# One transpose of 128x64 and eight row copies, in place of eight transposes of 128x8 and four copies

## What is computed

```python
xn = _layernorm(x, axis=-1)
q, k, v = split(xn @ W_attn + b_attn)          # 16 heads of 16
q = _apply_rope(q); k = _apply_rope(k)          # the angle goes by the head's number
att = einsum('bhqd,bhkd->bhqk', q, k) / 4.0
att = where(causal, att, -inf)
att = softmax(att, axis=-1)
s = einsum('bhqk,bhkd->bhqd', att, v) @ W_proj + b_proj
g = silu(silu(xn @ wg.T) * (xn @ wu.T) @ wd.T)  # int8 weights times 1/127
return x + s * g
```

## Time and profile before

| | us |
|---|---|
| three runs, median | 1255.55 |
| three runs, lowest and highest | 1254.56, 1260.43 |
| profiled execution, span from its first to its last instruction | 1257.5 |
| PE busy in the span | 1197.4 |
| DVE, ACT, POOL busy | 1013.0, 935.2, 693.3 |

### The profile page before, as it was taken

One profiled execution on the slowest core, in us unless ns is written; L12 is line 12 of the kernel. 1 busy time (PEld: TensorE's weight loads), 2 busy tenths in 40 slices (PEclk: granted clock), 3 DMA queues, 4 the chain that ended last, 5 costly groups with the idle time before them and its releaser, 6 DMA issues.

```text
span 1257.5 us, 29932 instructions
## 1 busy us (share of the span) xinstructions
PE 1197.4 (95%) x11324; PEld 558.3 (44%) x11324; DVE 1013.0 (81%) x2098; ACT 935.2 (74%) x1736; POOL 693.3 (55%) x863
## 2 busy tenths in 40 slices
PE   3889999999999999999999999999999999999986
PEld 2334444545345443544445453454445444454433
DVE  6678988888888888888888888888888888878732
ACT  4447777787877878778777878778787787778774
POOL 4527544395535937177453946369371874446472
PEclk9879999999999999999999999999999999999999
DMA  6140020401222120400204011221204002120101
GB/s 170 47 136 2 2 86 19 119 19 60 53 72 74 35 88 32 119 19 27 85 31 115 20 63 48 86 66 30 91 28 119 19 27 86 39 73 29 42 2 51
DMA packets 56004, 73.23 MB, mean 58 GB/s; under 512 B 8398, under 2 KB 34452, under 8 KB 55860
## 3 DMA queue, kind: packets, MB, share of 16 engines
q1 hardware_dynamic: 55848, 71.30, 18.9%
q10 hardware_dynamic: 12, 0.01, 0.0%
HBM read 44.96 MB, written 25.17 MB: 56 GB/s over the span
## 4 chain that ended last, share of the span: by engine, by line
PE 74%; POOL 10%; DVE 6%; issue 4%; ACT 4%; SPq 1%; DMA 1%; POOLq 0%; DVEq 0%; ACTq 0%
PE ring L854 31%; PE acc L845 17%; PE st L781 11%; PE ring L809 8%; PE ring L927 2%; DVE mx_a L1218 2%; POOL hf L1542 2%; PE ring L824 2%; ACT pexp L1055 2%; POOL hT L1551 1%; PE ring L864 1%; POOL xn L535 1%; PE ring L963 1%; POOL pexp L1512 1%; PE ring L942 1%
## 5 line engine op out<-in xcount | busy, mean ns | idle before, releaser
L1055 ACT ACTIVATE pexp<-st 128x512 f32<-128x512 f32 x1152 | 623.8, 598 | 124.0 <-PE st L781 123.3
L1218 DVE TENSOR_REDUCE mx_a<-ring 128x1 f32<-128x512 f32 (+2 forms) x960 | 536.8, 611 | 50.9 <-PE ring L809 26.0
L1512 POOL TENSOR_SCALAR_AFFINE_SELECT pexp<-pexp 128x512 f32<-128x512 f32 x256 | 158.4, 638 | 412.9 <-ACT pexp L1055 412.9
L845 PE MATMUL acc<-pexp,v_pad 128*17 128x512 f32 (+3 forms) x3072 | 303.7, 490 | 5.8 <-POOL pexp L1512 4.5
L809 PE MATMUL ring<-k_st,q_st 56*128 56x512 f16 (+4 forms) x1536 | 231.4, 326 | 13.3 <-POOL k_st L1641 3.4
L781 PE MATMUL st<-q_st,k_st 58*128 58x512 f16 (+3 forms) x1536 | 231.9, 331 | 6.1 <-ACT pexp L1055 3.4
L1218 DVE TENSOR_REDUCE mx_b<-ring 128x1 f32<-128x384 f32 (+2 forms) x448 | 210.4, 528 | 25.5 <-PE ring L824 24.7
L781 PEld LDWEIGHTS st<-q_st,k_st 58*128 58x128 f16 x1536 | 61.3, 93 | 265.2 <-ACT pexp L1055 173.4
L1542 POOL TENSOR_TENSOR hf<-ga,ups 128x512 f32<-128x512 f32 x96 | 122.4, 1275 | 42.0 <-issue 41.5
L845 PEld LDWEIGHTS acc<-pexp,v_pad 128*17 128x17 f32 x3072 | 61.9, 96 | 129.1 <-issue 105.7
L1551 POOL TENSOR_TENSOR hT<-hf,hT 128x512 f16<-128x512 f32 x96 | 111.4, 1161 | 3.4
(11 more groups left out here) (152 smaller groups left out, 1536.2 us busy)
## 6 DMA issues: line engine op xcount, KB each, us to landing
parts_scratch<-parts SPq DMA_DIRECT2D x32, 512.0 KB, 2.8
q_st<-parts_scratch SPq DMA_DIRECT2D x186, 64.0 KB, 2.2
k_st<-parts_scratch SPq DMA_DIRECT2D x186, 64.0 KB, 2.2
xo<-in_x SPq DMA_DIRECT2D x32, 256.0 KB, 2.9
out<-xo SPq DMA_DIRECT2D x32, 256.0 KB, 2.2
xn<-in_x SPq DMA_DIRECT2D x7, 1024.0 KB, 6.1
q_st<-mT SPq DMA_DIRECT2D x126, 4.0 KB
xn<-in_x SPq DMA_DIRECT2D x2, 512.0 KB, 6.2
```

Of the source, the lines that this page charges most:

```text
L845: mm = nc.tensor.matmul(acc[32 * j:32 * j + D + 1, CH - w:CH], v_pad[:, kb, GH * g + j, :], pexp[:, GH * (m % NSET) + j, at:at + w], start ...
L1055: nc.scalar.activation(pexp[:, GH * (n % NSET) + j, :], st[:, (GH * n + j) % NST, :], ACT.Exp, scale=1.0 / (QK_SCALE * np.sqrt(D))).then_i ...
L1218: top_ = nc.vector.reduce_max(dst, src, AX.X)
L1512: nc.gpsimd.affine_select(out=t, in_=t, compare_op=ALU.is_ge, fill=0.0, base=0, pattern=[[0, GH], [1, P]], channel_multiplier=-1).then_inc ...
```

## The change

`mx_p` is laid out with the tile of tokens as its innermost index instead of its outermost. Heads, parts and tiles together are 64 columns, and one transpose of 128x64 turns them all. ACT then copies 64 partitions of 128 instead of 8 partitions of 1024. A row of 1024 is now spread over 8 partitions of `mT`, so each row leaves in a DMA of its own, from 8 partitions into one: eight DMAs for a unit instead of four, and `mrow_in` counts to twice as much.

```diff
-        mx_p = sb("mx_p", [P, TT, GH, 2], fp16)
-        mT = sb("mT", [2 * GH, T], fp16)
+        mx_p = sb("mx_p", [P, GH, 2, TT], fp16)
+        mT = sb("mT", [2 * GH * TT, P], fp16)
@@ rows_of_maxima
-                eng.dma_start(q_st[row:row + 2, g, jj % 2, :], mT[2 * jj:2 * jj + 2, :]).then_inc(mrow_in[g], 16)
+                for part in range(2):
+                    first = (2 * jj + part) * TT
+                    eng.dma_start(q_st[row + part:row + part + 1, g, jj % 2, :].rearrange("o (t n) -> o t n", t=TT),
+                                  mT[first:first + TT, :]).then_inc(mrow_in[g], 16)
@@ scores, on PE
-                    pe.wait_ge(mrow_in[g], 16 * GH * (i + 1))
+                    pe.wait_ge(mrow_in[g], 16 * 2 * GH * (i + 1))
@@ task MT, on PE
-                    for tt in range(TT):
-                        mm = nc.tensor.transpose(dst[0:2 * GH, :].bitcast(fp16)[:, tt * P:(tt + 1) * P],
-                                                 mx_p[:, tt, :, :].rearrange("p j a -> p (j a)"), ident16[:, :])
-                    mm.then_inc(ready, 1)
+                    nc.tensor.transpose(dst[0:2 * GH * TT, :].bitcast(fp16)[:, 0:P],
+                                        mx_p[:, :, :, :].rearrange("p j a t -> p (j a t)"), ident16[:, :]).then_inc(ready, 1)
@@ task MT, on ACT
-                        act.wait_ge(mrow_in[(t[1] - 1) % GROUPS], 16 * GH * (i + 1))
-                    nc.scalar.activation(mT[:, :], src[0:2 * GH, :].bitcast(fp16), ACT.Copy)\
+                        act.wait_ge(mrow_in[(t[1] - 1) % GROUPS], 16 * 2 * GH * (i + 1))
+                    nc.scalar.activation(mT[:, :], src[0:2 * GH * TT, :].bitcast(fp16)[:, 0:P], ACT.Copy)\
@@ split_maxima, on DVE
-                m_t = m.rearrange("p a j t -> p t (a j)")
+                m_t = m.rearrange("p a j t -> p (a j) t")
-                nc.vector.tensor_scalar(mx_p[:, :, :, 0], m_t, -1.0 / M_UNIT, None, ALU.mult).then_inc(mp_chain, 1)
+                nc.vector.tensor_scalar(mx_p[:, :, 0, :], m_t, -1.0 / M_UNIT, None, ALU.mult).then_inc(mp_chain, 1)
-                nc.vector.scalar_tensor_tensor(out=mx_p[:, :, :, 1], in0=m_t, scalar=-1.0 / M_UNIT,
-                                               in1=mx_p[:, :, :, 0], op0=ALU.mult,
+                nc.vector.scalar_tensor_tensor(out=mx_p[:, :, 1, :], in0=m_t, scalar=-1.0 / M_UNIT,
+                                               in1=mx_p[:, :, 0, :], op0=ALU.mult,
```

## The result

| | median us (runs) | ratio to before | 95% interval |
|---|---|---|---|
| before | 1258.76 (10) | | |
| changed | 1262.55 (10) | 1.0046 | 1.0028 to 1.0064 |
| changed, measured again (e8 below) | 1262.23 (8) | 1.0049 | 1.0032 to 1.0067 |

The predicted 1249.7 and the range up to 1260 are missed. With ten runs the kernel before stands 3 us above the median of three on which the forecast was built, but its ratio, 0.995, is missed just as well. The two profiled executions have spans of 1257.5 and 1264.8.

What follows compares the result with a forecast made beforehand. PE, busy 95% of the span, was taken as the bound. A gain of 0.83 us a batch over seven batches, 5.8, with the ends summing to 0.0, took 1255.55 to 1249.7 us; the range was 1243.5 to 1260.

Steps and rivals of the forecast that it cites:

- The transposes: On PE, seven fewer transposes save 0.39 us a task; after holds in some slots, 0.83 a batch, 5.8 in seven batches.
- The rival that the saving does nothing: DVE and ACT set the pace of every batch and the 0.39 us vanish in waits: 1255.5 us; chance 0.04.
- the one that it passes in full: Rival: DVE's holds are soft, 28 × 0.39 = 10.9 us arrive, with the ends 1244 us; chance 0.12.
- ACT's copy: On ACT, the copy of 64 partitions of 128 takes 0.27 us, saving 0.73; counts only where PE or the rows wait.
- DVE's split: On DVE, as many elements in another order and no wait changed; costed at nothing.
- the pace of the issues: On SP's queue, the eight row copies' issues follow each other by 0.66 us.
- X: Time from a unit's first row-copy issue to its last landing: 3.2 us before, taken as 6.1, bounds 5.7 and 7.2.
- the time to land: From the last row copy's issue to its landing, read from the last packets: at most about 1.4 us, taken as 1.45.
- the rooms 6.26 and 6.19: Time in us from first row-copy issue to PE's start of the unit; no loss as long as X stays under 6.19.
- somewhat late: Rival: rows come with X 6.3 to 7.0, giving 1252.8 us at 6.4, 1256 at 6.6, 1263.5 at 7.0; chance 0.21.
- The last batch: Slot 16 gains 0.86 us, its unit gives 0.34 back, slot 27's unit ends 1.03 later; with the prologue 0.0.
- The slower rival: Eight issues cost what prologue copies from 8 partitions cost, X = 7.2, PE loses 1.48 a batch: 1268 us; chance 0.13.

Runs made afterwards that it cites:

- e8: The changed kernel measured once more, with nothing altered; 1262.23 us, ratio 1.0049 to the kernel before.
- e1: The changed kernel, but a unit's rows leave in four DMAs instead of eight; 1250.03 us, ratio 0.9933 to the kernel before.
- e6: The changed kernel with four row DMAs and the one transpose made eight times into the same place; 1255.61 us, ratio 0.9991 to the kernel before.
- e4: The changed kernel, but with four row DMAs for the last unit of the last batch only, eight elsewhere; 1255.93 us, ratio 0.9985 to the kernel before.
- e3: The changed kernel with eleven unused matmuls filling PE's wait at the last unit of the last batch; 1258.85 us, ratio 1.0019 to the kernel before.
- e2: The kernel before, but its rows leave in eight DMAs of one row from one partition each; 1278.24 us, ratio 1.0171 to the kernel before.
- e5: The changed kernel with two row DMAs a unit, each from 32 partitions; 1252.48 us, ratio 0.9955 to the kernel before.
- e7: The changed kernel with eight row DMAs for the last unit of the last batch only, four elsewhere; 1254.4 us, ratio 0.9981 to the kernel before.

## Why the prediction was wrong

**What bounds the kernel** was read rightly: PE does, and an edit counts by when PE can start.

**The transposes** were right. 0.39 a task was the gain where nothing holds PE, and 0.83 a batch what should pass. e1's seven batches give 5.3/7 = 0.75, and e6 takes all of it back. By the slots it was less exact: after the first issue PE starts the units of slots 18, 27 and 0 by 0.15, 0.30 and 0.17 sooner in e1 than in e6, where I had 0.25, 0.39 and 0.19. The rival that the saving does nothing and the one that it passes in full (1.56 a batch) are both out.

**ACT's copy, DVE's split, the pace of the issues, the last packet** were right: 0.26 for 0.27, 0.68 a step for 0.66, X = 6.1 to 6.2 for the 6.1 taken.

**The step that failed first is the time to land, 1.45 in X.** "Landing takes at most about 1.4" was read from the last packets, and then used as if PE could start at that moment. It starts 0.37 later, 1.74 after the last issue. So what has to be compared with the rooms 6.26 and 6.19 of slots 18 and 27 is 6.52, and not 6.1. That turns 0.1 to spare into waits of 0.26 and 0.33, 4.1 us in seven batches, and by the same formula a gain of 5.8 into one of 1.7. With 6.52 for X in all of its terms the prediction's sum gives 1254.7, a ratio of 0.9993, so this step takes nearly all of the gain, but it alone makes nothing slower and does not leave the range. I gave "somewhat late" 0.21, when the one number that decided it had been read at the wrong end.

By the laps the eight copies cost 4.8 (e4 against e1), 5.4 (e8) and 6.1 (changed) in the seven batches. The regular part of that is smaller than the formula's 4.1: in e1, where nothing waits, PE starts the units of slots 18 and 27 at 6.35 and 6.28 after the first issue, so they miss 6.52 by 0.17 and 0.24, 2.9 in seven batches. An undisturbed batch agrees: the second one takes 146.0 in the changed kernel, e4 and e8, and 145.6 in e1. The other 2 to 3 us are the disturbances below.

The Trainium skill ("DMA: Bandwidth & Descriptors", Anatomy of one DMA) says that the fixed cost of a DMA lies mostly in its completion, between the last byte and the semaphore, for DMAs that GpSimd issues and with HBM as the worst target. Here, on SP's queue and into SBUF, 0.37 us are seen behind the last packet, of 1.74 from the last issue to PE's start. So that part is there, but it is not most of the time.

**What was missing altogether are the disturbances.** The forecast took eight equal steps and one time to land. In the changed profile three of the 28 tasks of the middle have an issue of 1.0 to 1.4. This is the one at 436.02 (it should take 5.41), and the unit behind it, on the timeline of SP's queue and of PE:

```profile
436.02 6.14 SPq L598 DMA_DIRECT2D q_st<-mT  x8
443.40 0.39 PE L784 MATMUL st<-q_st,k_st 58*128 58x512 f16 x2 [0.95 <-DMA q_st<-mT]
```

And these are two of the DMA queues in the stretch from 440 to 442 (packets, MB, share of 16 engines):

```profile
q8 instruction: 1, 0.02, 3.9%
q1 hardware_dynamic: 48, 0.01, 2.1%
```

One packet of 16 KB of instructions holds one of the sixteen DMA engines for 3.9% × 16 × 2 us = 1.25 us, at just that time. The packets beside it are those of the rows. All three long issues have such a packet beside them, and the units behind them wait 0.95, 0.31 and 0.08. The largest wait of the seven batches has no long issue. It is in batch 0:

```profile
110.23 5.41 SPq L598 DMA_DIRECT2D q_st<-mT  x8
118.18 0.39 PE L784 MATMUL st<-q_st,k_st 58*128 58x512 f16 x2 [1.38 <-DMA q_st<-mT]
```

The eight issues take their 5.41, but PE starts 3.17 after the last one began, in place of 1.74. An instruction packet lies from 115.42 to 116.76. Of each of the last two row copies seven pieces start by 115.67 and 116.36, and the eighth only at 116.74 and 116.80. PE starts another 1.35 behind the last of them, where it is 0.37 elsewhere; what takes that long is open. e8 and e3 have the same wait with 1.0 and 0.9, e4 has none. The waits of 1.38, 0.95, 0.49 and 0.31 are 3.1 of the 5.4 us that PE waits for rows in the seven batches (with the waits of under 0.15 us, which the chain of waits leaves out).

That it is the instruction packet which delays an issue is seen by place only, and no run here moves it. It is also not enough by itself: in the changed kernel such a packet starts during the issues of 14 of the 28 units, and three have a long issue. In e1 it does so in seven and in the kernel before in three, and no issue there takes over 0.65. So those kernels, which also had over 2 us to spare, did not have to hide a long issue; they had none. In e2 nine issues of the seven batches take 0.87 to 1.85, each with a packet beside it. Why eight copies meet it and four do not is open.

The Trainium skill says of such loads of instructions ("Runtime: NRT & Kernel Launch", Instruction fetch mechanics) that their cost is mostly hidden. In the kernel before and in e1 no unit waited beside one; with eight copies some did.

**The last batch was priced without the clock.** I had 1.03 us for the unit of slot 27. With 0.37 for the start of PE and the 0.4 by which the unit's MT came later than forecast, since PE's savings up to there were used up, it comes to the measured 1.86 (1213.68 − 1211.82; counted from the last MT of each kernel it is 1.81). But the wait of 2.47 that this means for PE was never written down, and nothing in the sum asked what PE does after so long a pause. The falls of the clock cost another 5.3: 3.2 to 3.9 right behind this pause, and 1.6 behind the pause of 1.68 that all kernels have. The clock is the larger part of the miss at that place, and e3 shows it by itself. This term, put at nothing without a reason, is the second step that failed, and it and the disturbances are what makes the kernel slower than before and takes it out of the range.

**Put together**, against e1, in the laps: 5.4 to 6.1 in the seven batches, 0.6 in the next stretch, 2.5 for the last wait, 5.3 for the clock, 14 us in all, of which the 1.6 of the second fall are not shown to come from the change; timed, 1.0046 − 0.9933 is 1.1%, 14 us. Against the kernel before, the 5.3 won by the transposes and the 1.9 won behind the seven batches (1.2 and 0.7) are taken off: 7.4 and 6.6 us by the laps of its two executions, 5.8 (3.5 to 8.1) timed.

**The rivals.** The slower rival named the right mechanism, eight issues that come too late, but with a price an issue that was too high (0.735, measured 0.68), 2.1 to land (1.37, and 0.37 to PE's start) and nothing for the clock. It gave 1268. The copies that it took its prices from move 32 KB each, sixteen times a row of 2 KB and not four times, so they were a more distant neighbour than the prediction says. The better version lies in its name: keep the one transpose, and don't double the copies. e1 does so.

## What to carry to other kernels

A transfer is late or in time by the moment at which the waiting engine starts, not by its last packet: take the former from a place where an engine does wait for such a transfer, and if there is none, add a bound for it. If little room is left (here none), add a term for disturbances, since each now reaches the engine that sets the time; here they were 0.3 to 1.4 us, four times in seven batches. When a change makes the matrix engine pause for as long as here, 2.2 to 2.8 us, count with a granted clock of half behind the pause, here for 3 to 10 us; filling the pause with matmuls that compute nothing won that back. And a new layout does not have to bring new DMAs: one access pattern could carry two rows from sixteen partitions, at 0.65 us for 0.62.

## What the runs showed of the hardware

- From the last packet of a row copy to the start of the waiting matmul: 0.37 us, the same in the middle and at the end of the run.
- An issue on SP's queue: 0.563 us with two rows from two partitions, 0.589 with one row from one, 0.635 with one row of 8 pieces, 0.611 with two rows of 16 pieces, 0.616 with four rows of 32 pieces (e5). The number of DMAs sets the time, the pieces hardly.
- The granted clock: 1.00 to 0.50 behind the PE pause of 2.5 to 2.8 us ahead of the last unit, in each of the four profiled executions that had it (changed, e2, e7, e8). It was back at 1.00 after 10.2 us in three of them and after 6.8 in e2. Behind the pause of 2.2 in slot 9 of the last batch of e2 it fell for 3.4 us. Behind the pause of 1.68 it fell for 3.4 us in e5 and in both executions of the changed kernel and stayed at 1.00 in the seven others.
- A packet of 16 KB of instructions took one DMA engine 1.25 us (changed kernel, 440.5). Beside another, one piece of a row copy started 1.1 us after the seven others (116.74 against 115.67).
- The prologue, where PE pauses often, took 103.7 and 109.9 us to the same mark in two executions of one kernel, and the granted clock from 40 to 60 us differed as well:

```profile
40.00:60.00 20.00, 15.87 (x106) 6.42 (x104) 12.96 (x24) 9.12 (x15) 9.07 (x8) 0.91 0.12 35
60.00:80.00 20.00, 14.61 (x83) 5.87 (x77) 14.37 (x29) 6.27 (x11) 7.84 (x7) 0.88 0.36 119
```

```profile
40.00:60.00 20.00, 14.70 (x105) 6.61 (x103) 14.47 (x28) 7.14 (x12) 11.14 (x9) 1.00 0.28 83
60.00:80.00 20.00, 14.72 (x77) 5.14 (x76) 14.89 (x28) 8.54 (x15) 4.61 (x4) 0.77 0.33 107
```

The first pair is the changed kernel's first execution, the second is e8. This is where the 7.2 us between the spans of the two profiles compared here come from: their seven batches agree within 0.7 and their ends within 0.2. So the whole span of one execution says little on a change of 5 us; the laps say it.
